# More streaming matmuls in the second half of the two experts stages of a one-core network kernel

## What is computed

```python
logits = einsum('bsd,ed->bse', x, gate_w) + gate_b          # 16 experts
probs = softmax(logits, axis=1)
vals, idx = top_k(probs.transpose(0, 2, 1), 8)              # 8 positions per expert
pooled = einsum('bked,bke->bed', gathered, topv)            # weighted sum of the chosen positions
h = gelu(einsum('ebd,edh->ebh', [pooled, 1], weight1))      # first linear layer, 128 hidden
out = einsum('ebh,eho->ebo', [h, 1], weight2)               # second linear layer
outputs = zeros.at[batch, flat_idx].add(out * topv)         # back to the chosen positions
```

## Time and profile before

| | |
|---|---|
| median of three runs | 977.65 us (977.24, 977.65, 981.64) |
| the profiled execution, its own time | 977.46 us |
| its span, first to last instruction | 975.7 us (1.8 us lie around it) |
| PE busy | 906.0 us, 93% |
| DVE, ACT, POOL busy | 414.5, 446.3, 239.3 us |
| mean granted clock of PE | 0.976 of full |
| L1 experts, second half | from 371.4 to 380.3 us of the span |
| L3 experts, second half | from 961.3 to 970.1 us of the span |

### The profile page before, as it was taken

One profiled execution on the slowest core, in us unless ns is written; L12 is line 12 of the kernel. 1 busy time (PEld: TensorE's weight loads), 2 busy tenths in 40 slices (PEclk: granted clock), 3 DMA queues, 4 the chain that ended last, 5 costly groups with the idle time before them and its releaser, 6 DMA issues. The chain is left out here.

```text
span 975.7 us, 15499 instructions
## 1 busy us (share of the span) xinstructions
PE 906.0 (93%) x6268; PEld 517.4 (53%) x6268; DVE 414.5 (42%) x714; ACT 446.3 (46%) x1498; POOL 239.3 (25%) x144
## 2 busy tenths in 40 slices
PE   7958888888989989899999999999999999999987
PEld 4417766677754444444444444445555544554543
DVE  5599999999966655500000000002005400202763
ACT  4677777777735432233333333333333333333642
POOL 3239999999820000200000000000000000000410
PEclk9979999999999997899999999999999999999988
DMA  3020000000000000200000000000000000000000
GB/s 81 9 57 1 1 1 1 1 1 1 1 3 5 1 24 11 82 1 1 1 1 1 1 1 1 1 1 1 1 1 1 1 1 1 1 1 2 1 25 11
DMA packets 10220, 8.30 MB, mean 9 GB/s; under 512 B 7246, under 2 KB 8510, under 8 KB 10052
## 3 DMA queue, kind: packets, MB, share of 16 engines
q1 hardware_dynamic: 10148, 7.31, 3.0%
HBM read 5.47 MB, written 0.26 MB: 6 GB/s over the span
## 5 line engine op out<-in xcount | busy, mean ns | idle before, releaser
L909 PE MATMUL L2p_z<-stream 128*128 128x512 bf16 x943 | 366.7, 390 | 0.0
L951 ACT ACTIVATE L2yx<-L2p_z 32x2 f32<-32x2 f32 x1024 | 165.0, 161 | 323.3 <-PE L2p_z L928 323.2
L928 PEld LDWEIGHTS L2p_z<-L2yx,L2v 64*32 64x32 f32 x2048 | 137.6, 104 | 224.7 <-ACT L2yx L951 218.5
L928 PE MATMUL L2p_z<-L2yx,L2v 64*32 64x2 f32 x2048 | 225.5, 178 | 1.0 <-PEq L825 0.9
L789 POOL TENSOR_TENSOR hc<-hs,cb 128x1024 f32<-128x1024 f32 x64 | 149.6, 2365 | 4.8 <-DVE hs L730 4.8
L559 PEld LDWEIGHTS p_y<-ident,hc 128*128 128x128 f32 x1024 | 123.4, 192 | 15.6 <-POOL hc L789 7.8
L1642 DVE COPY xn_one<-L2yx 32x512 f32<-32x512 f32 (+1 forms) x2 | 0.8, 384 | 302.7 <-ACT L2yx L951 302.7
L559 PE MATMUL p_y<-ident,hc 128*128 128x128 f32 x1024 | 125.2, 276 | 4.0 <-POOL hc L789 4.0
L1642 POOL COPY xn_one<-L2yx 32x128 f32<-32x128 f32 x1 | 0.3, 283 | 484.2 <-SPq L1985 484.2
L730 DVE TENSOR_TENSOR_SCAN hs<-d_a,p_bb 128x1024 f32<-128x1024 f32 x48 | 109.8, 2287 | 6.6 <-ACT p_bb L659 0.5
L909 PEld LDWEIGHTS L2p_z<-stream 128*128 128x128 bf16 x943 | 90.1, 96 | 15.1
(11 more groups left out here) (524 smaller groups left out, 898.3 us busy)
## 6 DMA issues: line engine op xcount, KB each, us to landing
y_l<-in_pick SPq DMA_DIRECT2D x1, 768.0 KB
b_parts<-part SPq DMA_DIRECT2D x6, 128.0 KB, 2.4
c_parts<-part SPq DMA_DIRECT2D x6, 128.0 KB, 2.4
pos<-in_pos SPq DMA_DIRECT2D x1, 512.0 KB, 3.6
ao<-in_at_o SPq DMA_DIRECT2D x1, 512.0 KB, 4.2
L1w<-in_L_w SPq DMA_DIRECT2D x1, 297.0 KB
L3w<-in_L_w SPq DMA_DIRECT2D x1, 297.0 KB
x_tok<-in_x SPq DMA_DIRECT2D x2, 128.0 KB, 3.0
```

What stands on the lines that cost most here:

```text
L909: pe.matmul(p_z[:, 1, 0:each], stream[:, 0:128], stream[:, 0:each], start=True, stop=True)
L928: pe.matmul(p_step[:, t % 2], v[:, 0:C], yx[:, NB * t:NB * (t + 1)], start=True, stop=True).then_inc(s("preact"), 1)
L951: act.activation(yx[0:C, NB * (t + 1):NB * (t + 2)], p_step[:, t % 2], ACT.Sigmoid).then_inc(s("state"), 1)
```

## The change

Each of the two experts blocks gets fills at five places: three instead of two behind the first linear layer, one ahead of the sixth and one ahead of the eleventh of the 16 matmuls of the second layer, two instead of one ahead of the turn, four instead of two ahead of the spread, and nine instead of four at the end. That is 11 fills more per block.

```diff
                     last.then_inc(s("hidden"), 1)
-                    fill(2)
+                    fill(3)
                     pe.wait_ge(*at("gelu", 1))
                     for e in range(E):
+                        if e in (E // 3, 2 * E // 3):
+                            fill(1)
                         last = pe.matmul(p_e[:, 2 * e:2 * e + 2], w2[:, e], hid[:, 2 * e:2 * e + 2], start=True, stop=True)
                     last.then_inc(s("expert_out"), 1)
-                    fill(1)
+                    fill(2)
                     pe.wait_ge(*at("biased", 1))
                     pe.transpose(p_r, outs[:].rearrange("p b e -> p (b e)"), ident[0:C, 0:C]).then_inc(s("out_turned"), 1)
-                    fill(2)
+                    fill(4)
                     pe.wait_ge(*at("outb", 1))
                     for h, c in halves():
                         pe.matmul(p_x[h], outb[:].rearrange("p b c -> p (b c)"), wt[:, c], start=True, stop=True).then_inc(s("spread"), 1)
-                    fill(4)
+                    fill(9)
```

## The result

The changed kernel took 984.61 us (median of 19 executions, 979.47 to 999.71) against 978.95 us for the kernel before on the same chip (median of 19, 976.08 to 985.69). The ratio is 1.0052, with a 95% interval from 1.0034 to 1.0071: 3.3 to 7.0 us slower. The forecast was 977.9 us in a range from 975.6 to 982.8; the time lies above it. Executions of one and the same kernel differ here by several us, those of the changed kernel by 20.

A forecast was written before the change was run, and what follows sets the result against it. The experts blocks' second halves were taken as a chain without slack, slowed by clock falls. L1 +0.62, equivariant norm -0.5, L3 +0.74, output -0.41: +0.45 on 977.46 gives 977.9 us, range 975.6 to 982.8.

The forecast's parts named there:

- (a): Behind each experts block's first layer: a third fill adds its full +0.22 us, lower bound +0.13.
- (b): Second layer of each experts block: two single fills cost +0.39 us each, +0.78 together, lower bound 0.43.
- (c): Ahead of the turn in each experts block: two fills for one cost +0.20 us, down to 0.09.
- (d): Ahead of the spread in each experts block: four fills for two cost +0.23 us, +1.04 at the half level.
- (e): Spread in each experts block: 0.88 us at full clock, saving 1.02 in L1 and 0.90 in L3.
- (f): End of each experts block: nine fills for four cost +0.21 us at full clock, +2.1 at the half level.
- if the clock holds: Likeliest case: full clock through the experts blocks' second halves and into the equivariant norm; forecast range (976.9 to 979.5) 0.48.
- (g): Equivariant block's norm behind L1: 5.50 us for 6.53 at full clock, -1.03 possible, -0.5 taken.
- rival B: Clock falls before the spread anyway: +4.3 us per block, 981.6 to 982.1 or near 986; chance 0.27 one block, 0.08 both.
- (h): Output's turn behind the L3 block: 0.68 us at full clock in place of 1.09, -0.41.
- rival C: Clock full through the whole equivariant norm and at the matmuls of lines: 976.7 us, down to 975.6; chance 0.13.
- D: Nothing happens: all new fills in the experts blocks fit in waits; no separate chance, others together 0.04.

The follow-up runs named there:

- tail_l1: Kernel before with nine fills in place of four at the end of the L1 experts block alone; 982.67 us, ratio 1.0029.
- tail_only: Kernel before with nine fills in place of four at the end of both experts blocks, nothing else; 983.66 us, ratio 1.0042.
- no_fills: Kernel before without any fill behind the first layer in both experts blocks; 979.00 us, ratio 0.9993.
- short_tail: Changed kernel with four fills at the end of each block in place of nine; 980.88 us, ratio 1.0027 to the kernel before.
- no_singles: Changed kernel without the two single fills amid the second layer; 982.17 us, ratio 1.0024 to the kernel before.
- middle_only: Kernel before with three, two and four fills at the three waits, no singles, four at the end; 978.50 us, ratio 0.9976.
- middle_no_tail: Kernel before with three, two and four fills at the three waits, no singles, none at the end; 982.02 us, ratio 1.0016.
- singles_all: Changed kernel with a single fill ahead of each of the last 15 second-layer matmuls, not two; 999.63 us, ratio 1.0200 to before.
- lean_again: Kernel before with one, none, one and two fills in place of two, one, two and four, second run; 979.27 us, ratio 0.9986.
- after_again: Changed kernel, unedited, measured a second time, six executions; 990.7 us, ratio 1.0138 to the kernel before.
- after: Changed kernel in its first comparison with the kernel before; median 984.61 us, ratio 1.0052, profiled execution 987.32 us.
- after_third: Changed kernel, unedited, measured a third time; 985.83 us, ratio 1.0065 to the kernel before; profiled execution 979.52 us.
- singles_only: Kernel before with the two single fills amid the second layer, nothing else; 981.33 us, ratio 1.0008.
- the middle runs: Two runs of the kernel before with three, two and four fills at the waits, four at the end; 978.50 and 980.54 us.

## Why the prediction failed

**Most prices were right.** Set against the pieces of the profiles (us; "two levels" is full and half; second layer by first and last pass):

| step | forecast | before, two levels | changed, two levels |
|---|---|---|---|
| (a) fills to second layer | +0.22 | 0.52, 0.95 | 0.74, 1.37 |
| (b) second layer | +0.78 | 1.00, 1.68 | 1.83, 2.94 |
| (c) last pass to turn | +0.20 | 0.44, 0.67 | 0.64, 1.09 |
| (d) turn to spread | +0.23; +1.04 at half | 0.81, 1.12 | 1.10, 1.98 |
| (e) spread | 0.88 at full | 1.01, 1.90 | 1.01, 1.90 |
| (f) tail | 2.40; 4.3 at half | 1.78, 2.18 | 2.41, 4.32 |
| first layer | none | 1.36, 2.42 | 1.36, 2.42 |
| block | | 6.9, 10.9 | 9.1, 16.0 |

At one level of the clock the change costs 2.2 us a block at full and 5.1 at the half level. (The block's rows of before are sums of these pieces; a block of before wholly at the half level is measured in the profile of tail_l1, 10.92 in L3.) That the new fills end every wait and are paid in full was right, and so was the price of a single fill, 0.41 (forecast 0.39): handing over to float32 weights is not hidden.

**The step that failed is the choice of the case: "if the clock holds", in the sum of (e), (f) and (g), taken as the likeliest.** It rested on the two places of the fall in one execution, and on the reading that the two thin linear layers make the clock fall and fills in them would hold it. The runs show that the places move from one execution to the next with the same list of instructions: the fall in L1 lay at about 376 in the profile of before and at 371.6 in that of the changed kernel, ahead of everything that was changed. It lay ahead of the first layer in L1 in nine of the 17 profiles (those of the changed kernel, tail_only, no_fills, short_tail, no_singles, middle_only, middle_no_tail, singles_all and lean_again), so it can come without the thin layers ahead of it. The changed kernel's own three profiles have the fall at 371.6, near 376 and not in the block at all.

The Trainium skill says as much of the clock's rise ("TensorE: Matmul & The Clock Gate", section "What's actually happening": where it comes varies from run to run, so one should not fit to one count); I cited that section and did not draw this from it. What it says is of the start of a kernel; that a fall inside one moves too is what these profiles show.

With the fall ahead of the first layer every new fill is paid at the half level, which rival B had only for (d) and (f): B came to +4.3 us over the block of the profile, L1 lost 7.7 in the profile after. With the fall near 376, where the profile of before has it too, B's own case came (after_again, +4.8 and +4.9): the new fills put the turn (376.77, before 375.35) and all the fills ahead of the spread behind that moment.

**A base that mixed the levels** hid the price of the tail. (f) was set against 2.19 us, a half-level figure, and came out at +0.21. At full clock four fills end with DVE's addition, 1.78, so nine cost +0.63; at the half level they cost +2.14. The tail was a small term of the forecast and is the largest of the loss: tail_only has 4.0 us by the means, against 0.5 for the singles and about nothing for the fills at the waits, each by itself.

**The prices of (g) and (h) were right**: 5.49 us for the norm with the clock back (forecast 5.50) and 0.68 for the output's turn. But the forecast took only half of (g), -0.5, and nothing behind the norm except in rival C. Both profiles of the changed kernel with the clock full through the norm have all of (g), -1.04 in after and -1.03 in after_third. Behind the norm, after gave back 0.75 more: 0.50 at the matmuls of lines, where the clock was still full, and 0.25 because DVE and no longer the 17 fills ends the block (16.26 in all, in place of 18.05). In after_third the clock fell at 387.5, ahead of those matmuls, and the block took 17.61.

```profile
398.70 0.24 DVE L1461 TENSOR_SCALAR rc<-e2p_r,eb 64x32 f32<-64x32 f32 x1 [0.88 <-PE e2p_r L1438]
```

(The wait for the matmuls of lines in after, 0.88 in place of 1.38 in the earlier trace rows.) The nine fills are not alone in this: the equivariant block takes 16.6 to 16.7 us in the profiles of no_fills, middle_only and singles_only too, which have none or four at the end. It depends on where the clock fell and came back.

**Even the forecast's case came out higher.** after_third, which had the clock full through both blocks, has a span of 977.7 us, 2.0 over that of before: +0.8 and +1.1 for the blocks (forecast 0.62 and 0.74; the spread's 1.01 in place of 0.88 is 0.13 of the difference in each, and L3's tail of 2.50 another 0.10), -0.44 for the equivariant block, -0.5 behind the L3 block (most of it the output's turn, -0.41), and +1.0 in stretches that the change leaves alone.

**Rivals.** B was the right side: its "both, near 986" is what after_again's profile shows at 986.22 us, by +4.8 and +4.9 where it had +4.3, and it has no case for a fall ahead of the first layer. C's mechanism, the clock full through the norm and at the matmuls of lines, was there in the profile after and in those of tail_l1 and tail_only (16.3 to 16.4 for the equivariant block), but its time was not, since the blocks ahead cost more. D is out. That extra fills change nothing in the clock, as the prediction read the idle rule of the Trainium skill ("TensorE: Matmul & The Clock Gate", section "What's actually happening"), is not borne out by these runs: over all, the changed kernel spent 47 us at the half level in place of 52, the middle runs 40 and 44 and no_singles 42. But this is not the simple rule "fills hold the clock" either, since taking all nine out of a block changed nothing (53 us). Added fills at the waits shortened the time at the half level, and it did not pay.

**What stays open.** The parts by themselves add up to some 5 us (means), the whole change is 5 to 13 over before. Seven of its 34 executions were over 990 us (64 us at the half level) and none of the 138 of before. None of the seven was profiled. The profile of tail_l1, at 989.55 us, shows what such an execution can hold: 6.2 us from L3's norm to its fills at the half level, 2.8 in L3's second half and 2.6 in the attention part. Why the change should meet it more often was not shown. Nor can the profiles say how often each place of the fall comes, since each kernel has one, and the changed one three.

## What to carry to other kernels

A matmul that only keeps the clock up is free as long as it ends before the wait that it fills; check this at the lower clock, since that is where the kernel is when it has failed, and there it takes twice as long. Compare a stretch before and after at the same granted clock, and do not take the place of a fall in one profile as fixed: profile several executions, or price every place where it could lie. Ahead of a block's end, count what the slowest other engine still has to do, and put no more fills there than fit beside it (here at most four at full clock, where nine held the next block up by 0.6 to 2.1 us).

## What was not expected

A whole second half without a fill (no_fills), at the half level from end to end, is as fast as one with nine: 9.5 us for the L1 block against 10.9 at the same level, ratio 0.9993 for the kernel. And 15 fills among 32 thin passes, with PE busy for 4.00 of every 4.00 us, left the clock at its lower level from 372 to 392 us of the span.
